# Sorting the edges of a two-layer graph network on one core: where the counts, the slot decoding, the moments and the code bits are done

## The chip, the cores and the metric

One core of a Trainium2 chip. The metric is the device time of one execution in microseconds, here the median of several. Engines are called TensorE (PE; its weight loads are PEld), VectorE (DVE), ScalarE (ACT), GpSimd (POOL) and SyncE (SP, which here only issues transfers).

## The reference

1250 nodes with 512 features, 41250 edges (sources and targets in `src` and `dst`, sorted by `dst`), one weight an edge.

```python
h = jnp.maximum(_layernorm(x, axis=-1), 0.0)
m = relu(concatenate([h[src], h[dst]], axis=1) @ W0.T + b0)     # per edge
x = x + segment_sum(m, src, num_segments=1250)
h = jnp.maximum(_layernorm(x, axis=-1), 0.0)
out = segment_sum((h @ W1.T)[src] * edge_weight[:, None], dst, num_segments=1250)
x = x + where(out >= 0, out, alpha * out)
```

## The kernel before, in words

Nodes form 10 blocks of 125, edges lie as 125 rows by 330 columns. The kernel first sorts the edges into tiles of 128 by the pair (block of the source, block of the target), 100 buckets; this is the part that the change touches. Then come the edge groups and mixed groups, which build the messages of a tile and sum them into nodes and into a 1250 x 1250 matrix M of weights, and at last the second layer's products and the output. These later stages start behind the barrier at the end of the sort and are the same in both kernels.

**The prelude of the sort.** VectorE turns node numbers into block numbers and digits (`dig_s`, `dig_d`: one-hot over blocks, L529). ScalarE regroups them, TensorE makes a histogram (L768) and totals (L773), VectorE works out the first slot of each bucket from them by a chain of some twenty short instructions (L562 to L593). The 330 columns are five chunks of 66. For each chunk `count` (L671 to L681, 66 matmuls) makes the counts of the buckets by column, ScalarE copies them to `counts_out` (`copy_counts`, L823), SyncE moves them to one row a bucket (`counts_by_bucket`, L331), VectorE runs a scan over them (`bases`, L441, with the running value of the chunk before) and splits the result in two halves, which SyncE writes as two rows into `hot`; a third row, `base_up`, comes from ScalarE. `hot_of_block` (L434) fills the other rows of `hot`. TensorE's `prefix` (L683) then gives, seven buckets at a time and 15 times a chunk, the slot of each edge in each bucket; VectorE's `pick` (L457) keeps that of the edge's own bucket, and `slots` (L473) adds the picked planes and decodes tile and lane by eleven short instructions, each of which waits for the one before. In the prelude this is done for chunk 0.

Beside it, in the prelude: VectorE makes the bits of an edge's code (L603 to L611), GpSimd the pieces of its weight (L396 to L398) and the bias rows; ScalarE the moments of x (`moments`, L874: two blocks early, eight between the first and the second half of the weights) and their square roots with one table load; TensorE turns the first layer's weights (`turn_w`, L709, eight) and takes off their rounded part (`low_w`, L718, eight), with ScalarE's two copies of each (`turned_weights`, L884). Two pairs of weights come before chunk 0's prefixes and two behind. SyncE's queue has `src`, the first two blocks of x, the weights, the rest of x, the bias, alpha, and the clearing of the table in HBM, and then the counts and rows.

**The column loop.** Of the 330 columns, 136 (`DMA_COLS`) are scattered by GpSimd into a table in HBM, one indirect transfer each (L417), chunk by chunk as soon as the slots of the chunk are ready. The other 194 (`PE_COLS`: 38 in each of the first four chunks, 42 in the last) are placed by TensorE. Column q: VectorE makes two one-hots (`column`, L495), ScalarE three scaled pieces (`pieces`, L836; in 28 columns VectorE makes these too), TensorE three matmuls (`place`, L697). A ring of six buffers lets VectorE run up to six columns ahead of `place`. All the rest is hung into this loop by hand, by column number: within a chunk, at column i, the hot blocks of the next chunk (i below 10), a clearing of the planes (i = 10), its `bases` (i = 4), `prefix` (from 9), `pick` (from 14) and all of `slots` (30), and the counts of the chunk after next in three thirds near the chunk's end (`COUNT_BACK`), with ScalarE's copy at `COPY_BACK`; and by a period of 16 columns (`STEP`), one block of the first layer: normalizing, turning, eight steps of products, two roundings.

At the end SyncE reads the table back (L351), VectorE adds it to what TensorE placed (L655) and decodes, and a barrier ends the stage.

Of the kernel before, what the change touches and what calls it, by code (L numbers as in the profile page):

```python
# [20 lines left out]
ALU = mybir.AluOpType  # L21
ACT = mybir.ActivationFunctionType
# [8 lines left out]
P = 128  # L31
N = 1250
D = 512
# [51 lines left out]
BASES_AT, PREFIX_AT, PICK_AT, SLOTS_AT = 4, 9, 14, 30  # L85

COUNT_BACK, COPY_BACK = 7, 3


STEP = 16  # L90
NORMAL_AT, TURN_AT, ROUND_AT, REST_AT, PRODUCT_AT = 2, 5, 8, 12, 13
# [14 lines left out]
def build(nc, x, src, dst, edge_weight, w0, b0, w1, alpha, out):  # L106
    rows_dram = nc.dram_tensor("edge_rows", [2, AGRP, GRP * P], BF16).ap()
    table_dram = nc.dram_tensor("edge_table", [1 + P * NT, TABLE_FIELDS], F32).ap()
    with ExitStack() as top:
# [13 lines left out]
        neg_mean = sb("neg_mean", [P, NBLK], F32)  # L123
# [19 lines left out]
        with ExitStack() as early:  # L143
# [22 lines left out]
            ones_row = early_sb("ones_row", [EROWS, NBKT], F32)  # L166
            own_base = early_sb("own_base", [NBKT, NBKT], F32)
# [9 lines left out]
        with ExitStack() as scope:  # L177
# [32 lines left out]
            ones_r = sb1("ones_r", [2, P], F32R)  # L210
            before_b = sb1("before_b", [P, P], BF16)
            keep = sb1("keep", [NBKT, CHUNK + 1], BF16)
            counts_out = sb1("counts_out", [NBLK, NBLK, CHUNK], BF16)
            counts = sb1("counts", [NBKT, CHUNK + 2], BF16)
            running = [sb1(f"running{k}", [NBKT, CHUNK + 1], F32) for k in range(2)]
            base_hi = sb1("base_hi", [NBKT, CHUNK], BF16)
            base_lo = sb1("base_lo", [NBKT, CHUNK], BF16)
            bases_at = sb1("bases_at", [NBKT, 2], F32)
# [9 lines left out]
            bias_r = sb1("bias_r", [2, D], F32R)  # L228
# [3 lines left out]
            sums = sb1("sums", [BN, 3, NBLK], F32)  # L232
# [7 lines left out]
            HALF = CHUNK // 2  # L240
            def count_ps(k):

                return [psum[0:NBLK, bank, 0:HALF * NBLK] for bank in ((0, 2) if k == 1 else (4, 5))]

# [17 lines left out]
            code_ready = sem("code_ready")  # L262
            digits_ready = sem("digits_ready")
# [14 lines left out]
            counts_in = sem("counts_in")  # L278
# [18 lines left out]
            act_own = sem("act_own")  # L297
            std_ready = sem("std_ready")
            rstd_ready = sem("rstd_ready")
# [15 lines left out]
            with nc.Block() as block:  # L315
                @block.sync
                def _(sp):
                    for rows in SPLIT:
                        sp.dma_start(src_i[rows], src.rearrange("(p c) -> p c", p=EROWS)[rows]).then_inc(src_in, 16)
                    for part, blocks in enumerate(X_PARTS):  # L320
                        for rows in SPLIT:
                            sp.dma_start(S[rows, blocks], x.rearrange("(b p) d -> p b d", p=BN)[rows, blocks]).then_inc(x_in[part], 16)
                        if part == 0:
                            sp.dma_start(w_in[:], w0.rearrange("(o p) i -> p o i", p=P)).then_inc(w_loaded, 16)
# [3 lines left out]
                    sp.wait_ge(cleared, 1)  # L328
                    sp.dma_start(table_dram[1:1 + P * NT].rearrange("(p t) f -> p (t f)", p=P),
                                 zeros.rearrange("p t f -> p (t f)")).then_inc(cleared_dram, 16)  # L330
                    def counts_by_bucket(k):  # L331
                        sp.wait_ge(count_out, k + 1)
                        if k > 0:
                            sp.wait_ge(scan_step, k)
                        sp.dma_start(counts[:, 2:CHUNK + 2], counts_out[:]).then_inc(counts_in, 16)

                    counts_by_bucket(0)
                    for k in range(NCHUNK):
                        for r, part in enumerate((base_hi, base_lo)):
                            sp.wait_ge(base_rows, 2 * k + r + 1)  # L340
                            sp.dma_start(hot[EROWS + r:EROWS + r + 1], part[:]).then_inc(rows_in, 16)
                        if k == 0:
                            sp.wait_ge(upper_row, 1)
                            sp.dma_start(hot[EROWS + 2:EROWS + 3], base_up[:]).then_inc(upper_in, 16)
# [1429 lines left out]
```

## Time and profile before

| what | us |
|---|---|
| median of 3 runs | 1008.88 (1006.73 to 1010.54) |
| the profiled execution, its own time | 1017.97 |
| its span | 1016.2 |
| mean granted TensorE clock | 0.975 |
| TensorE busy | 972.9 (96%) |
| VectorE busy | 872.2 (86%) |
| ScalarE busy | 775.0 (76%) |
| GpSimd busy | 643.0 (63%) |

The durations come from the profiled execution, which was 9.1 us longer than the median. Matmuls are pipelined and the ends of their records are modelled, so TensorE's busy share says less than the starts of its instructions. A row of a timeline gives the start, the length up to the end of the last of the merged instructions, the engine, the line, the operation, and in brackets how long the engine sat idle before it and what released it. Issuing a transfer is shown with a q behind the engine. In a row of waits stand the total, the times and the longest. The sort ends at 276.65 us of the span, the first column is placed at 52.76.

### The profile page before, as it was taken

To read this page: it belongs to the slowest core of one execution; us is meant where nothing else is said; L and a number is where in the kernel's file an instruction comes from. 1 tells how busy PE (TensorE), PEld (TensorE's weight loads), DVE (VectorE), ACT (ScalarE), POOL (GpSimd) and SP (SyncE) were. 2 spreads that over 40 slices of the span, in tenths; PEclk is the share of its full clock that TensorE was granted. 3 is DMA by queue.
4 is the path that set the end of the run, shared out by engine and by line. 5 is a ranking of instruction groups with operands and counts; after the bars stand their busy time and mean duration, and the time that the engine had idled before them with its cause. 6 is when DMAs were issued, how large, how long until landed. Compare 5 with 4: busy or idle time off the path is not lost.

```text
span 1016.2 us, 20178 instructions
## 1 busy us (share of the span) xinstructions
PE 972.9 (96%) x4719; PEld 781.0 (77%) x4720; DVE 872.2 (86%) x1747; ACT 775.0 (76%) x1650; POOL 643.0 (63%) x934
## 2 busy tenths in 40 slices
PE   5799999999799999999999999999999999999998
PEld 5477778787678887788878778878888788778776
DVE  6989988897769999999999999999999888873444
ACT  4887878778788888888888888888888776755210
POOL 2478877767477777777777777777777755530000
PEclk9689999899989999999999999999999999999999
DMA  8000000000021111111111111111111100010011
GB/s 220 4 3 4 2 4 2 4 2 3 19 62 42 44 42 41 40 42 43 41 43 42 40 40 41 43 42 41 44 41 42 31 30 30 24 42 1 21 41 40
DMA packets 35923, 35.16 MB, mean 35 GB/s; under 512 B 7778, under 2 KB 32095, under 8 KB 35876
## 3 DMA queue, kind: packets, MB, share of 16 engines
q1 hardware_dynamic: 31176, 33.95, 10.7%
q0 software_dynamic: 4416, 0.30, 1.7%
q8 instruction: 23, 0.38, 0.2%
q10 hardware_dynamic: 284, 0.33, 0.1%
q14 instruction: 24, 0.20, 0.1%
HBM read 30.92 MB, written 3.29 MB: 34 GB/s over the span
## 4 chain that ended last, share of the span: by engine, by line
PE 68%; DVE 2%; ACT 1%; issue 1%; POOL 0%; POOLq 0%
PE node_ps L1166 8%; PE edge_ps L1205 8%; PE edge_ps L1211 8%; PE edge_ps L1210 8%; PE edge_ps L1206 8%; PE node_ps L1167 8%; PE m_ps L1177 4%; PE psum L1309 3%; PE psum L1311 3%; PE psum L1310 3%; PE m_ps L1291 1%; PE edge_ps L1269 1%; PE edge_ps L1270 1%; PE edge_ps L1261 1%; PE edge_ps L1266 1%; PE edge_ps L1265 1%
## 5 line engine op out<-in xcount | busy, mean ns | idle before, releaser
L1398 ACT ACTIVATE msg_hi<-edge_ps 128x512 fp32r<-128x512 f32 x332 | 197.6, 595 | 60.8 <-PE edge_ps L1211 60.7
L1122 POOL TENSOR_TENSOR M<-M,pair_w 125x125 f32 x332 | 160.7, 484 | 126.9 <-DVE pair_w L1545 97.2
L1559 DVE SCALAR_TENSOR_TENSOR msg_lo<-edge_ps,msg_hi 128x512 fp32r<-128x512 f32 x332 | 223.6, 683 | 17.3 <-ACT msg_hi L1398 13.0
L417 POOL DMA_INDIRECT edge_table<-fields,row_no x136 | 170.4, 1253 | 58.2 <-issue 47.4
L844 ACT ACTIVATE lane_piece<-hot_lane,fields 125x128 fp32r<-125x128 bf16 x498 | 153.8, 392 | 12.1 <-DVE hot_lane L504 11.8
L705 PE MATMUL psum<-hot_tile,lane_piece 125*128 125x384 f32 x582 | 145.8, 373 | 9.2 <-ACT lane_piece L844 6.3
L1106 POOL TENSOR_TENSOR hot_w<-hot_d,weight_l 128x252 fp32r<-128x252 bf16 x166 | 140.0, 843 | 0.0
L1166 PE MATMUL node_ps<-msg_hi,hot_s 128*125 128x512 f32 x332 | 135.1, 407 | 0.0
L1205 PE MATMUL edge_ps<-b_hi,turned_d 125*128 x332 | 132.7, 400 | 0.7 <-ACT turned_d L1382 0.7
L1211 PE MATMUL edge_ps<-a_lo,turned_s 125*128 x332 | 131.9, 397 | 0.0
L1210 PE MATMUL edge_ps<-a_hi,turned_s 125*128 x332 | 131.4, 396 | 0.2 <-ACT turned_s L1382 0.2
L1206 PE MATMUL edge_ps<-b_lo,turned_d 125*128 x332 | 131.3, 395 | 0.0
L1167 PE MATMUL node_ps<-msg_lo,hot_s 128*125 128x512 f32 x332 | 130.7, 394 | 0.0
L705 PEld LDWEIGHTS psum<-hot_tile,lane_piece 125*128 125x128 f32 x582 | 106.1, 196 | 30.6 <-ACT lane_piece L844 17.1
L1373 ACT ACTIVATE square<-spread,minus_no 125x512 bf16<-125x512 bf16 x164 | 117.8, 718 | 2.7
L1540 DVE TENSOR_TENSOR S<-S,node_ps 125x512 f32 x166 | 112.7, 679 | 1.5
L502 DVE TENSOR_SCALAR hot_tile<-iota,tile_no 125x384 fp32r<-125x384 f32 x194 | 89.8, 463 | 20.6 <-PE psum L705 17.8
L1106 POOL TENSOR_TENSOR hot_w<-hot_d,weight_h 128x252 fp32r<-128x252 bf16 x166 | 101.3, 610 | 4.1 <-DVE hot_d L1550 3.1
L1390 ACT COPY pair_w<-m_ps 125x504 f32<-125x504 f32 x166 | 94.6, 570 | 0.0
L1545 DVE TENSOR_TENSOR pair_w<-pair_w 125x252 f32<-125x252 f32 x166 | 86.3, 520 | 0.0
L1166 PEld LDWEIGHTS node_ps<-msg_hi,hot_s 128*125 128x125 f32 x332 | 61.6, 185 | 25.8 <-issue 13.1
L1550 DVE TENSOR_TENSOR hot_s<-iota_h,local_s 128x504 fp32r<-128x504 f16 x96 | 75.5, 787 | 0.0
(258 smaller groups left out, 2044.8 us busy)
## 6 DMA issues: line engine op xcount, KB each, us to landing
spread<-edge_rows SPq DMA_DIRECT2D x190, 125.0 KB
out_dram<-result SPq DMA_DIRECT2D x10, 224.0 KB
edge_table<-fields,row_no POOLq DMA_INDIRECT x136
w_in<-in_L_gnn_W_dram SPq DMA_DIRECT2D x1, 2048.0 KB, 12.7
S<-in_x_dram SPq DMA_DIRECT2D x1, 1792.0 KB
w_in<-in_L_gnn_W_dram SPq DMA_DIRECT2D x1, 1024.0 KB, 5.1
S<-in_x_dram SPq DMA_DIRECT2D x1, 448.0 KB
edge_table<-zeros SPq DMA_DIRECT2D x1, 384.0 KB, 14.9
```

The costliest lines, as they stand in the source:

```text
L417: pool.indirect_dma_start(table_dram[:, :], bass.IndirectOffsetOnAxis(ap=row_no[:, c:c + 1], axis=0), fields[:, c, 0:TABLE_FIELDS], None). ...
L705: mm = pe.matmul(code_ps if f == 0 else weight_ps, lane_piece[r][:, f, :], hot_tile[r][:], start=(q == 0 and f < 2), stop=True, skip_group ...
L1106: pool.tensor_tensor(hot_w[h][:, :, f, :], hot_d[k][:, 0, h * PAIR:(h + 1) * PAIR, :], part[:, bass.ds(g * GRP + (MIXC + h * PAIR), PAIR)] ...
L1122: pool.tensor_tensor(part, part, pair_w[h][:, j, 0, 0:BN], ALU.add).then_inc(m_added, 1)
L1166: pe.matmul(sums[:], hot_s[k][:, j, 0:BN], msg_hi[j][:], start=(j % PAIR == 0), stop=False)
L1167: pe.matmul(sums[:], hot_s[k][:, j, 0:BN], msg_lo[j][:], start=False, stop=(j % PAIR == PAIR - 1)).then_inc(tile_summed, 1)
L1205: pe.matmul(edge_ps[j][:], td, b_hi[:, b_rows], start=True, stop=False)
L1206: pe.matmul(edge_ps[j][:], td, b_lo[:, b_rows], start=False, stop=False)
L1210: pe.matmul(edge_ps[j][:], ts, a_hi[:, a_rows], start=False, stop=False)
L1211: pe.matmul(edge_ps[j][:], ts, a_lo[:, a_rows], start=False, stop=True).then_inc(edge_ready, 1)
L1398: act.activation(msg_hi[j][:], edge_ps[j][:], ACT.Relu).then_inc(hi_ready, 1)
L1559: dve.scalar_tensor_tensor(out=msg_lo[j][:], in0=edge_ps[j][:], scalar=0.0, in1=msg_hi[j][:].bitcast(F32), op0=ALU.max, op1=ALU.subtract). ...
```

## The change

Counts and bases. All counts get room of their own (`counts_out`, `counts`, `running` over all 330 columns). The counts of chunks 2, 3 and 4 are made behind columns 0, 1 and 2 of chunk 0 (`COUNTS_AT`), copied by ScalarE two columns later, always as two halves; the bases of chunk 1 are scanned at column 1, those of chunks 2 to 4 in one scan of 198 columns at column 12 (`BASES_AT`). SyncE writes the rows of a chunk when the picks of the chunk before are done. Prefixes start at column 8 and wait only for the hot blocks that they read.

Slots. `slots` is cut into ten steps, two a column, from column 30 to 34; the wait for the last is at the chunk's last column. The first pick of a later chunk is a product of prefix and one-hot, so that the planes aren't cleared.

Moments. VectorE makes them with two statistics instructions a block, and the reciprocal and shift block by block; block 0 in the prelude, block b at stages 2, 3, 11 and 12 of the 16 columns before its own; ScalarE takes one root a block, and its table for roots is loaded at the start.

Code bits. GpSimd makes them in nine instructions instead of VectorE's five, from the moment the pairs are known, and then the weight pieces as before.

Order. The weights are loaded on ScalarE's queue, the table is cleared from GpSimd's, the rest of x is loaded behind chunk 0's rows of bases. After the first pair of weights, TensorE does one of the twelve other parts of weights behind each of prefixes 1 to 12. The bias is multiplied with 128 rows instead of 2, of which all but two are zero.

```diff
-BASES_AT, PREFIX_AT, PICK_AT, SLOTS_AT = 4, 9, 14, 30
-COUNT_BACK, COPY_BACK = 7, 3
+WEIGHTS_FROM, COUNTS_AT, COPIES_BEHIND = 1, (0, 1, 2), 2
+BASES_AT, PREFIX_AT, PICK_AT, SLOTS_AT = (1, 12), 8, 14, 30
+SLOT_STEPS, STEPS_A_COLUMN = 10, 2
+MOMENTS_AT, STD_AT = (2, 3, 11, 12), 4
...
                     counts_by_bucket(0)
-                    for k in range(NCHUNK):
...
+                    counts_by_bucket(1)
+                    rows_of_bases(0)
+                    sp.wait_ge(upper_row, 1)
+                    sp.dma_start(hot[EROWS + 2:EROWS + 3], base_up[:]).then_inc(upper_in, 16)
+                    load_x(1)
+                    rows_of_bases(1)
+                    for k in range(2, NCHUNK):
+                        counts_by_bucket(k)
+                    for k in range(2, NCHUNK):
+                        rows_of_bases(k)
...
+                    pool.wait_ge(pairs_ready, 1)
+                    pair_of, part, upper_bits = blk_a[:, 1, :], local[:, 1, :], local[:, 0, :]
+                    own(pool.tensor_scalar(part, node_f[:, 0, :], float(TILE), None, ALU.mult))
+                    own(pool.tensor_tensor(upper_bits, part, node_f[:, 1, :], ALU.add))
...
+                        if k > 0 and g == 0:
+                            dve.tensor_tensor(planes[:, 0:nb, :].rearrange("p b c -> p (b c)"), psum[0:EROWS, 3 + n % 3, 0:nb * CHUNK],
+                                              hot[0:EROWS, 0:nb, :].rearrange("p b c -> p (b c)"), ALU.mult).then_inc(picked, 1)
...
+                    def moment(b, stage):
+                        if stage == 0:
+                            dve.wait_ge(x_in[0 if b < X_PARTS[0].stop else 1], 32)
+                            dve.bn_stats(stats[:, b, :], S[0:BN, b, :]).then_inc(moments, 1)
+                            return
+                        dve.wait_ge(moments, 4 * b + stage)
+                        if stage == 1:
+                            dve.bn_aggr(mv[:, b, :], stats[:, b, :]).then_inc(moments, 1)
...
-                    weights(1)
                     for g in range(NPICK):
                         prefix(0, g)
-                    weights(2)
-                    weights(3)
+                        if WEIGHTS_FROM <= g < WEIGHTS_FROM + 12:
+                            weights_part(4 + g - WEIGHTS_FROM)
...
-                            part = i - last + COUNT_BACK
-                            if k + 2 < NCHUNK and 0 <= part < 3:
-                                count(k + 2, range(CHUNK // 3 * part, CHUNK // 3 * (part + 1)))
+                            if k == 0 and i in COUNTS_AT:
+                                count(COUNTS_AT.index(i) + 2)
```

## Rows read from the trace of the kernel before

**Rows 1.** The page, part 4: the chain that ended last, shares by engine.

```profile
PE 68%; DVE 2%; ACT 1%; issue 1%; POOL 0%; POOLq 0%
```

**Rows 2.** Busy time by stretch of the column loop; PE, PEld, DVE, ACT, POOL, PEclk.

```profile
86.64:132.31 45.67, 43.60 (x268) 36.10 (x268) 41.67 (x119) 38.46 (x117) 34.89 (x28) 1.00 0.09 3
132.31:179.12 46.81, 44.34 (x268) 36.70 (x267) 40.12 (x119) 38.52 (x117) 35.26 (x28) 0.96 0.08 3
179.12:227.68 48.56, 47.28 (x272) 38.95 (x271) 41.90 (x120) 38.70 (x118) 35.79 (x28) 0.93 0.08 3
227.68:271.94 44.26, 42.35 (x204) 33.83 (x202) 34.87 (x101) 37.98 (x122) 29.81 (x24) 1.00 0.10 11
```

**Rows 3.** Timeline of TensorE before the first column: start us, us, instruction.

```profile
29.70 0.85 PE L693 MATMUL psum<-hot,before_b 128*125 128x462 bf16 x3 [1.44 <-DMA hot<-base_up]
...
46.05 3.79 PE L714 MATMUL psum<-ident,w_in 128*128 128x128 f32 x16 [0.19 <-ACT w0T_lo L890]
...
49.49 0.77 PE L721 MATMUL psum<-w0T_hi,minus_ident 128*128 128x512 f32 x1
...
52.76 2.99 PE L705 MATMUL psum<-hot_tile,lane_piece 125*128 125x384 f32 x9 [1.65 <-issue]
```

**Rows 4.** Timeline of ScalarE, the same stretch.

```profile
42.46 1.28 ACT L906 ACT_TABLE_LOAD   x1
...
51.63 2.74 ACT L844 ACTIVATE lane_piece<-hot_lane,fields 125x128 fp32r<-125x128 bf16 x9
```

**Rows 5.** Timeline of VectorE, the same stretch.

```profile
24.78 0.36 DVE L447 TENSOR_TENSOR_SCAN running<-keep,bases_at,counts 100x67 f32<-100x67 bf16 x1 [4.24 <-DMA counts<-counts_out]
...
30.12 8.10 DVE L469 COPY_PREDICATED planes<-hot,psum 125x462 f32<-125x462 uint16 x15 [0.32 <-PE psum L693]
...
38.25 1.90 DVE L480 TENSOR_REDUCE slot<-planes 125x66 f32<-125x924 f32 x1
...
42.41 0.23 DVE L492 SCALAR_TENSOR_TENSOR row_no<-lane,tile_no 125x66 int32<-125x66 f32 x1
```

**Rows 6.** Timeline of SyncE's DMA issues, the same stretch.

```profile
16.18 0.94 SPq L335 DMA_DIRECT2D counts<-counts_out  x1
...
26.99 0.74 SPq L344 DMA_DIRECT2D hot<-base_up  x1
```

**Rows 7.** GpSimd's weight pieces and first scatter; all scatters of the loop grouped.

```profile
31.59 1.05 POOL L398 TENSOR_TENSOR fields<-weight,fields 125x330 f32<-125x330 f32 x1
...
43.66 1.29 POOL L417 DMA_INDIRECT edge_table<-fields,row_no  x1 [7.47 <-issue]
...
L417 POOL DMA_INDIRECT edge_table<-fields,row_no x131 | 164.0, 1252 | 49.6 <-issue 38.7 <-DVE row_no L492 10.9
```

**Rows 8.** End of the loop: SyncE's read of the table, its wait, VectorE's first use.

```profile
266.19 0.34 SPq L351 DMA_DIRECT2D raw<-edge_table  x1
...
SPq L315 <- DMA raw<-edge_table: 2.5, 1, 2.5
...
271.94 0.56 DVE L655 TENSOR_TENSOR raw<-raw,psum 128x384 f32<-128x384 f32 x1 [2.78 <-PE psum L705]
```

**Rows 9.** GpSimd beside a two-input VectorE instruction, and after it.

```profile
277.41 0.97 POOL L1106 TENSOR_TENSOR hot_w<-hot_d,weight_h 128x252 fp32r<-128x252 bf16 x1 [3.09 <-DVE hot_d L1550]
...
278.91 0.60 POOL L1106 TENSOR_TENSOR hot_w<-hot_d,weight_h 128x252 fp32r<-128x252 bf16 x1
```

**Rows 10.** Counts in chunks one and two: ScalarE's wait, TensorE's wait, one third of counts.

```profile
140.11 0.70 ACT L833 CAST counts_out<-psum 10x660 bf16<-10x660 f32 x1 [3.04 <-remote]
...
142.21 0.79 PE L705 MATMUL psum<-hot_tile,lane_piece 125*128 125x384 f32 x3 [2.06 <-ACT lane_piece L844]
...
180.38 0.75 PE L678 MATMUL psum<-dig_d,dig_s 125*10 125x10 bf16 x22
```

**Rows 11.** Two microseconds behind the counts of chunk two, columns as in rows 2.

```profile
184.00:186.00 2.00, 2.00 (x5) 1.12 (x6) 1.68 (x7) 2.00 (x7) 1.39 (x3) 0.50 0.06 1
```

**Rows 12.** Statistics by VectorE in the last stage, grouped.

```profile
L1625 DVE BATCH_NORM_STATS2 stats<-S 125x6 f32<-125x512 f32 x10 | 6.8, 682 | 0.0
```

More of the change, by code:

```diff
@@ new lines, in slots @@
+                        dve.wait_ge(vstep, steps[0])
+                        if step == 1:
+                            mark(dve.tensor_scalar(quotient, slot[:], -MID_SLOT, 1.0 / UPPER, ALU.add, ALU.mult))
+                        if step == 2:
+                            mark(dve.tensor_scalar(upper, quotient, MAGIC, -MAGIC, ALU.add, ALU.add))
+                        if step == 3:
+                            mark(dve.scalar_tensor_tensor(out=slot[:], in0=upper, scalar=-UPPER, in1=slot[:], op0=ALU.mult, op1=ALU.add))
@@ new lines, in slots @@
+                        if step == 4:
+                            mark(dve.tensor_scalar(quotient, slot[:], -(TILE - 1) / 2, 1.0 / TILE, ALU.add, ALU.mult))
+                        if step == 5:
+                            mark(dve.tensor_scalar(whole, quotient, MAGIC, -MAGIC, ALU.add, ALU.add))
+                        if step == 6:
+                            mark(dve.tensor_tensor(after, whole, upper, ALU.subtract))
+                            mark(dve.scalar_tensor_tensor(out=at, in0=whole, scalar=-float(TILE), in1=slot[:], op0=ALU.mult, op1=ALU.add))
@@ new lines, in slots @@
+                        if step == 7:
+                            mark(dve.tensor_scalar(in_mix[:], after, float(MID_TILE), None, ALU.is_equal))
+                            mark(dve.scalar_tensor_tensor(out=tile, in0=after, scalar=float(MID_TILE), in1=whole, op0=ALU.is_le, op1=ALU.add))
+                        if step == 8:
+                            mark(dve.copy_predicated(tile, in_mix[:].bitcast(U16), mix_no[:, cols]))
+                        if step == 9:
+                            dve.scalar_tensor_tensor(out=row_no[:, cols], in0=at, scalar=float(NT), in1=tile, op0=ALU.mult,
+                                                     op1=ALU.add).then_inc(slots_ready, 1)
@@ L645, in _ @@
                                         pick(k + 1, g)
-                                if i == SLOTS_AT:
-                                    slots(k + 1)
+                                for step in range(SLOT_STEPS):
+                                    if i == SLOTS_AT + step // STEPS_A_COLUMN:
+                                        slots(k + 1, step)
+                                if i == FIRST[k + 1] - FIRST[k] - 1:
                                     dve.wait_ge(slots_ready, k + 2)
@@ L770, in _ @@
                     mm.then_inc(hist_done, 1)
[L771 removed]
+                    count(0)
                     pe.wait_ge(spread_done, 1)
```

267 lines of the change are left out of this document (122 added, 145 removed).

## The prediction

> **What bounds the kernel now.** I read the chain that ended last first [rows 1]: 68% of the span is TensorE's. The edge and mixed groups and the output blocks behind 276.65 us are not touched by the change, and I carry their time over unchanged. What can move is the sort: a prelude until the first column is placed, and 194 columns after it.
>
> In the column loop the table of busy time by stretch shows that no engine is far ahead [rows 2]. The four stretches go from one decoding of slots to the next, the last one to the end of the loop. TensorE is busy 42 to 47 us of each, but VectorE 40 to 42 and ScalarE 38 to 39 of the first three: whoever is late by more than the ring of six columns stops the others.
>
> The prelude is a relay. TensorE's first prefix starts at 29.70 [rows 3], with a wait for the row that SyncE loads last; the second half of the turned weights runs up to the first column at 52.76. ScalarE does the moments and a table load of 1.28 us at 42.46 before it copies these weights out, and only at 51.63 makes the first pieces of a column [rows 4]. VectorE waits 4.24 us for the first counts, picks from 30.12, reduces from 38.25 and issues the last step of the first decoding at 42.41, so ends it at 42.64 [rows 5]. On SyncE the counts are issued at 16.18, behind all of x, the weights and the clearing of the table; the last row of bases is issued at 26.99 [rows 6].
>
> One more engine must be read, though it never stops the others: GpSimd. It does the weight pieces from 30 us on, issues its first scatter at 43.66 and then 136 in all; those of the loop take (164.0 + 38.7) / 131 = 1.547 us each with the gap of issue, and only 10.9 us are waits for slots [rows 7]. The table is read back at 266.19 and has landed after 2.5 us of waiting, at about 269.0; VectorE needs it at 271.94, where TensorE's last column releases it [rows 8]. So GpSimd's chain has 2.9 us of slack at the end of the loop, and no more.
>
> **The change part by part.**
>
> *Transfers.* x's second part moves behind the first rows of bases on SyncE, the weights go to ScalarE's queue (one issue more, while ScalarE would wait for digits), the clearing of the table to GpSimd's (about 1 us of issue, in time that GpSimd has idle). The counts' transfer then has little ahead of it. I give it the 2.7 us that the last row took from its issue to the prefix it released (26.99 to 29.70) [rows 3, 6]: landed at 18.9. VectorE's wait of 4.24 [rows 5] goes to zero, and everything behind it in this relay moves by 4.2: first prefix at 25.5. The bound for this part is 0 (another load ahead still holds it) to -4.2.
>
> *Code bits by GpSimd.* Nine instructions of 125x330 at most 1.05 us each [rows 7], so 8 to 10 us from 13 us on; with the weight pieces done by 25, where nothing waits for them before the first column. VectorE loses five, 2.6 us, in a stretch where it waits for the prefix anyway: 0. What it may cost is the neighbour. An operation of GpSimd takes 0.97 us beside a VectorE instruction that reads two operands from SBUF, and 0.60 us alone [rows 9]; the loser here is GpSimd. The other direction isn't isolated by a row. VectorE has some 12 such short dependent instructions from 14 to 20.5 us. I take +1.0 us for all of them (a tenth of an operation each), with ends 0 and 12 x 0.5 = +6, half an operation each. First prefix: 26.5.
>
> The Trainium skill ("SBUF — State Buffer", Who interferes with whom) speaks against this placing: a VectorE instruction with two SBUF inputs and a GpSimd one that reads SBUF exclude each other for the whole instruction, and whoever issues first blocks the other. By that rule the upper end holds, and it is a rival below.
>
> *Weights between the prefixes.* This is the step that costs. Before, 15 prefixes were bound by the picks, 8.10 / 15 = 0.54 us each [rows 5], and twelve parts of weights came partly behind. Now all twelve parts lie between prefixes 1 and 13. Two turns take 49.49 - 46.05 = 3.44 us, six take 10.3; six roundings are shown at 0.77 alone, I take 0.5 each in a row, 3.0; a prefix takes 0.85 / 3 = 0.28, I take 0.33 with handovers, 5.0 [rows 3]. Sum 18.3 us (ends 16.0 and 10.3 + 4.6 + 8.1 = 23.0). The last prefix ends at 44.8, its pick at 45.3, and the decoding takes 42.64 - 38.25 = 4.4 [rows 5], nothing being there to lie between: 49.7, which is 7.1 us later than before. ScalarE's moments, table load and late weight copies [rows 4] fall away, so the first pieces no longer wait for them: decoding 49.7, about 0.8 for the first two one-hots (an estimate; GpSimd's first scatter, which the same decoding releases, came 1.0 behind it) [rows 7], pieces 1.1 (51.63 to 52.76) [rows 3, 4], first column placed at 51.6 against 52.76. The gain of the prelude is 1.2 us for TensorE, and a loss of 7.1 us for GpSimd.
>
> *Counts.* Three sets (198 matmuls) leave the ends of chunks 0 to 2 and go behind columns 0 to 2. A third of a set is 0.75 us [rows 10], a set 2.1. At the loop's start ScalarE gives a column each 2.74 / 3 = 0.91 us [rows 4], and TensorE waits for it; my estimate is that 2 or 3 of the 6.4 us fill this idle time, and that ScalarE's three copies, queued ahead of its next pieces, add a little. I take +3.0 for the first stretch (ends +1, +5). In chunk one ScalarE waited 3.04 us for its copy of the counts and TensorE 2.06 for the pieces then missing [rows 10]; behind the counts of chunk two the clock fell to the lower level, 0.50 granted (1.2 of 2.4 GHz) [rows 11]; three windows of 2 us in a row look like this one, so some 3 us were lost. Taken from the first three stretches of [rows 2]: counts 2.1 + 2.1 + 2.1, TensorE's stall 2.1, the clock 1.1 (half may come back elsewhere). That is 9.5, and the ends are 6 and 12.
>
> *Slots in ten steps, picks.* The eleven instructions behind the reduction take 42.64 - 40.15 = 2.5 us, each waiting for the one before [rows 5]; spread, I take half, -1.2. The first pick of a chunk multiplies and so needs no clearing, and two of three scans are merged away with their roundings: about -1.2 (an estimate, at 0.36 for a scan [rows 5]). *Moments:* statistics take 0.68 us a block [rows 12], with three small ones about 1.1, and a chunk has 38 / 16 blocks: +2.6. VectorE comes out even; I take 0 (ends -3, +3). The bias product with 128 rows instead of 2 streams as many columns: 0.
>
> *Sum.* TensorE: 51.6 + (271.9 - 52.8) + 3.0 - 9.5 = 264.2. GpSimd: first scatter 1.0 behind the decoding, at 50.7; 136 x 1.547 = 210.4, no wait for slots since a chunk of 28 takes it 43.3 us; end 261.1, read 1.2 later, landed 2.8 after: 265.1. **The two ends are within 1 us of each other**, GpSimd's is the floor, and any slip of either counts, so I take 266.5, against 271.94: -5.4 us. The profiled execution took 1017.97 (span 1016.2 and 1.8 around it), 9.1 above the median 1008.88; its changed twin would take 1012.6. The same difference on the median gives **1003.5 us**. About 0.5%, 5 us, is what a measurement of this kernel can tell from no change, so this forecast lies at the edge.
>
> **The rivals.**
> *A shorter prelude.* If prefixes and roundings take their lower ends (16.0) and the neighbour costs nothing, decoding ends at 46.4, GpSimd at 261.8 and TensorE with 12 us saved at 260: about -9.5, 999.4. For it: TensorE is then never idle; against it: the clock stood at the lower level there before.
>
> *The port.* VectorE's chain is held by 6 instead of 1 us: decoding ends at 54.7, GpSimd's chain at 270.1: -1.8 and 1007.1. For it is the rule above, against it that the rows show GpSimd as the one delayed.
>
> *VectorE or ScalarE bounds the loop.* The counts' time is not given back, as VectorE's 40 us a chunk, its wait at column 12 for the transfers of three counts and the ring of six columns set the pace: 4 of the 9.5 us are saved, the loop ends at 269.7: -2.2, 1006.7. For it: VectorE's busy time is within 2 to 5 us of TensorE's [rows 2].
>
> *Slower: the scatters.* GpSimd starts 7 us later and now has no slack. If VectorE's denser stream stretches its cycle, every 0.1 us costs 13.6. From 1.60 us on the gain is gone; at 1.65 the chain ends at 50.7 + 224.4 + 4.0 = 279.1, +7.2 and 1016.1. For it: GpSimd's busy time of 28 scatters rose from 34.89 to 35.79 over three chunks; against it: that is 0.03 us each [rows 2].
>
> **How the numbers follow.** Forecast 0.50 (1001 to 1005.5; 0.36 beyond 0.5%, 0.14 within), shorter prelude 0.10, port 0.15, VectorE's bound 0.13, scatters 0.12. Faster 0.36 + 0.10 = 0.46; same 0.14 + 0.15 + 0.13 = 0.42; slower 0.12. The range takes in the forecast, port, VectorE's bound and most of the shorter prelude, with 1 to 2 us of scatter between runs: 998 to 1011. It leaves out the slower scatters and the far end of the short prelude.
>
> **What would show it.** The first scan of bases near 20.6 without a wait; first prefix at 25 to 27; turned weights between prefixes and the last prefix near 45; first scatter near 50.7, scatters without waits for slots, and the table's arrival, not TensorE's last column, as what releases VectorE near 266; no stall at the counts in chunk one. The forecast is wrong if the first scatter comes later than 55, if the mean cycle of the scatters is above 1.6, or if TensorE's last column ends behind 268.

## The result, and the profile after

| | median, us | lowest to highest | runs |
|---|---|---|---|
| kernel before | 1009.47 | 1005.21 to 1012.43 | 20 |
| changed kernel | 1012.60 | 1010.07 to 1014.19 | 20 |

Ratio 1.003, 95% interval 1.002 to 1.0041: slower by 3.1 us, or 0.3%. The forecast of 1003.5 had the wrong sign, and the result lies outside its range. The profiled execution of the changed kernel took 1012.84 us (span 1011.1, mean clock 0.981) and is typical of its runs. That of the kernel before took 1017.97, 5.5 above the longest of these 20 runs. So a second and a third profile of the kernel before were taken (`before_again`, 1008.76 us, and `before_third`, 1011.44). The rows below are set against `before_again`, in places against `before_third` too.

Busy time by stretch of the changed kernel, columns as in [rows 2]: from one decoding of slots to the next, the end of the loop, the stage behind the barrier.

```profile
49.23:93.20 43.97, 42.43 (x364) 36.93 (x365) 40.52 (x120) 35.14 (x110) 34.43 (x28) 0.83 0.10 5
93.20:134.76 41.56, 39.59 (x196) 33.21 (x195) 41.39 (x126) 37.67 (x118) 33.33 (x27) 1.00 0.08 3
134.76:177.06 42.30, 40.28 (x204) 33.77 (x202) 41.89 (x127) 38.76 (x120) 34.07 (x28) 1.00 0.09 3
177.06:218.18 41.12, 40.74 (x206) 35.42 (x207) 40.66 (x124) 38.03 (x118) 33.19 (x27) 1.00 0.08 3
218.18:266.88 48.70, 39.19 (x192) 31.98 (x190) 32.76 (x93) 34.78 (x113) 35.72 (x29) 0.95 0.10 10
...
271.88:1011.10 739.22, 727.41 (x3310) 581.30 (x3310) 638.25 (x1069) 558.61 (x1007) 459.24 (x765) 0.99 0.12 38
```

The same table of `before_again`:

```profile
81.36:126.41 45.05, 43.31 (x268) 36.09 (x268) 40.93 (x119) 38.58 (x117) 36.21 (x29) 1.00 0.09 3
126.41:172.06 45.65, 44.21 (x272) 36.27 (x272) 41.33 (x119) 38.71 (x117) 36.81 (x29) 1.00 0.09 3
172.06:219.24 47.18, 45.44 (x271) 37.60 (x270) 41.90 (x121) 38.46 (x117) 38.03 (x30) 0.96 0.09 3
219.24:263.52 44.28, 42.05 (x202) 33.47 (x200) 34.83 (x101) 38.01 (x122) 29.80 (x24) 1.00 0.10 11
...
268.20:1007.10 738.90, 727.44 (x3310) 582.61 (x3310) 638.59 (x1069) 558.84 (x1007) 461.90 (x765) 0.99 0.12 38
```

The stage behind the barrier takes 739 us in both, so the difference is made in the sort. The three middle stretches did get shorter, by 3.5, 3.4 and 6.1 us (4.1, 3.3 and 4.4 against `before_third`). The first stretch, taken up below, is 10.8 us longer, and the last one 4.4: 48.7 us with 39.2 of TensorE's work in it. The end of the sort shows what holds the last one. Changed kernel: VectorE's first use of the table, TensorE's last columns, GpSimd's last scatter, SyncE's read of the table, and all scatters grouped as in [rows 7].

```profile
266.88 0.55 DVE L707 TENSOR_TENSOR raw<-raw,psum 128x384 f32<-128x384 f32 x1 [10.63 <-DMA raw<-edge_table]
...
245.89 12.72 PE L754 MATMUL psum<-hot_tile,lane_piece 125*128 125x384 f32 x60 [0.56 <-ACT lane_piece L885]
...
261.25 1.17 POOL L444 DMA_INDIRECT edge_table<-fields,row_no  x1 [0.30 <-issue]
...
263.83 0.36 SPq L360 DMA_DIRECT2D raw<-edge_table  x1
...
L444 POOL DMA_INDIRECT edge_table<-fields,row_no x136 | 171.7, 1262 | 61.0 <-issue 59.4 <-DVE row_no L535 1.6
```

And in `before_again`, with TensorE's first column ahead:

```profile
48.18 5.79 PE L705 MATMUL psum<-hot_tile,lane_piece 125*128 125x384 f32 x18 [1.65 <-ACT lane_piece L844]
...
263.52 0.56 DVE L655 TENSOR_TENSOR raw<-raw,psum 128x384 f32<-128x384 f32 x1 [2.81 <-PE psum L705]
...
250.74 12.74 PE L705 MATMUL psum<-hot_tile,lane_piece 125*128 125x384 f32 x60 [0.56 <-ACT lane_piece L844]
...
255.12 1.23 POOL L417 DMA_INDIRECT edge_table<-fields,row_no  x1 [0.31 <-issue]
...
257.76 0.34 SPq L351 DMA_DIRECT2D raw<-edge_table  x1
...
POOL edge_table L417 <- DVE row_no L492: 0.4, 1, 0.4
```

Before, TensorE's last column releases VectorE, at 263.5, and the table had landed 2.8 us earlier, at 260.7 (read issued from 257.76 to 258.10, then 2.6 of waiting). After, TensorE is done at 245.89 + 12.72 = 258.6, 4.9 earlier than in `before_again` and 7.1 earlier than in `before_third`, and VectorE then sits idle for 10.63 us, until the table is there. **The sort now ends at GpSimd's chain of 136 scatters**, whose end, the issue of the read behind the last scatter, moved from 257.8 to 263.8: 3.9 us by its later start (first scatter at 48.30, in `before_again` at 44.41), 1.2 by waits for slots (1.6 against 0.4) and 1.0 by the scatters themselves (from the first one's start to the last one's end, less these waits, 212.5 against 211.5). From there to the landing it is as long as before.

VectorE's first use of the table is thus the mark of every run below: 271.94 in the profile shown before [rows 8], 263.52 and 265.76 in the other two of the same kernel, 266.88 after. From the mark to the end of the span it was 740.9 to 744.3 us in the fourteen profiles of this document, so a difference between two marks gives that between two whole times only to within some 3 us.

The prelude of the changed kernel, where TensorE's rows answer to [rows 3]:

```profile
29.29 1.00 PE L742 MATMUL psum<-hot,before_b 128*125 128x462 bf16 x2 [3.08 <-DVE hot L464]
...
35.01 1.11 PE L763 MATMUL psum<-ident,w_in 128*128 128x128 f32 x8
35.95 0.36 PE L742 MATMUL psum<-hot,before_b 128*125 128x462 bf16 x1
...
41.63 0.42 PE L742 MATMUL psum<-hot,before_b 128*125 128x462 bf16 x2
49.23 1.30 PE L754 MATMUL psum<-hot_tile,lane_piece 125*128 125x384 f32 x3 [7.17 <-ACT lane_piece L885]
```

VectorE's scan, reduction and last decoding step, as in [rows 5], and GpSimd's first scatter, as in [rows 7]:

```profile
23.61 0.75 DVE L473 TENSOR_TENSOR_SCAN running<-keep,running,counts 100x66 f32<-100x66 bf16 x1
...
42.91 1.89 DVE L513 TENSOR_REDUCE slot<-planes 125x66 f32<-125x924 f32 x1
...
47.05 0.23 DVE L535 SCALAR_TENSOR_TENSOR row_no<-lane,tile_no 125x66 int32<-125x66 f32 x1
...
48.30 1.30 POOL L444 DMA_INDIRECT edge_table<-fields,row_no  x1 [18.59 <-issue]
```

The scan no longer waits for the counts but comes only 1.2 earlier than in [rows 5]; the prefixes end at 42.05, the slots are decoded at 47.28. TensorE has its first column at 49.23 (48.18 in `before_again`).

### The profile page after: what moved, and what is told of

Its sections match the earlier page's. It is cut to its first block, busy times and chain, and to the rows that moved or that the text cites. A ratio compares the mean times of both kernels' runs of the same rounds, so it can differ in the third digit from the quotient of the medians.

```text
span 1011.1 us, 20245 instructions
## 1 busy us (share of the span) xinstructions
PE 955.0 (94%) x4719; PEld 774.3 (77%) x4720; DVE 877.9 (87%) x1770; ACT 760.9 (75%) x1621; POOL 655.2 (65%) x946
## 4 chain that ended last, share of the span: by engine, by line
PE 69%; DVE 2%; ACT 1%; issue 0%; POOL 0%; POOLq 0%
PE node_ps L1190 8%; PE edge_ps L1234 8%; PE edge_ps L1229 8%; PE edge_ps L1235 8%; PE edge_ps L1230 8%; PE node_ps L1191 8%; PE m_ps L1201 4%; PE psum L1333 3%; PE psum L1335 3%; PE psum L1334 3%; PE m_ps L1315 1%; PE edge_ps L1293 1%; PE edge_ps L1294 1%; PE edge_ps L1289 1%; PE edge_ps L1285 1%; PE edge_ps L1290 1%
## 5 line engine op out<-in xcount | busy, mean ns | idle before, releaser
L545 DVE TENSOR_SCALAR hot_tile<-iota,tile_no 125x384 fp32r<-125x384 f32 x194 | 93.8, 483 | 8.5 <-PE psum L754 8.4
L1569 DVE TENSOR_TENSOR pair_w<-pair_w 125x252 f32<-125x252 f32 x166 | 84.0, 506 | 0.0
L1190 PEld LDWEIGHTS node_ps<-msg_hi,hot_s 128*125 128x125 f32 x332 | 61.5, 185 | 27.0 <-issue 13.6
## 6 DMA issues: line engine op xcount, KB each, us to landing
w_in<-in_L_gnn_W_dram ACTq DMA_DIRECT2D x1, 2048.0 KB, 11.9
```

Of the source, the lines that this page charges most:

```text
L1190: pe.matmul(sums[:], hot_s[k][:, j, 0:BN], msg_hi[j][:], start=(j % PAIR == 0), stop=False)
```

## The experiments

Ratios are to the kernel before on the same chip in the same session. Its medians were 1010.18 (beside `before_again`, `prefix_first`, `bits_vector`, `scatter_132`), 1008.50 (`slots_whole`, `before_132`, `counts_prelude`, `three`) and 1010.52 us (`bits_132`, `three_132`, `scatter_128`, `before_third`). Each variant was profiled once, so a mark is that of one execution.

### Is the first profile typical?

No edit: the kernel before again.

> The kernel before, unchanged, profiled once more. My theory: the profiled execution on which the prediction rests was an unlucky one (1017.97 us against 1005 to 1012 in 20 others), and the time lost lay in the column loop (TensorE's stall and two stretches at the lower clock). Expected: an execution of 1007 to 1011 us, VectorE's first use of the table (line 655) at 262 to 266 us instead of 271.9, little or none of the lower clock between 140 and 192 us, and behind the barrier 739 to 740 us again. Rival: the sort takes as long as in the first profile and the difference lies behind the barrier or around the span; then line 655 stands near 271 us again.

> The kernel before, unchanged, profiled a third time. Theory: the column loop of the kernel before ends where TensorE's columns end, and this varies from execution to execution by some us with stalls and with the stretches at the lower clock; VectorE's first use of the table at 261 to 267, execution 1006 to 1012 us, the stage behind the barrier 739 to 740 us. Rival (the first profile was typical of profiled executions): 270 us or more, and 1015 us or more.

Measured 1008.76 and 1011.44 us; the first use of the table came at 263.52 and 265.76, both times released by TensorE, with waits for slots of 0.4 and 4.1 us in place of 10.9. So 8.4 of the 9.1 us between the first profile's span and that of `before_again` lie ahead of that use: 4.6 ahead of TensorE's first column (52.76 in [rows 3], 48.18), the rest in the loop. Three stretches show the loss, columns as in [rows 2]. First the profile shown before, then `before_again`:

```profile
46.05:49.49 3.44, 3.44 (x17) 3.44 (x17) 3.30 (x12) 1.02 (x2) 2.83 (x3) 0.50 0.07 1
...
132.00:148.00 16.00, 13.91 (x116) 10.96 (x115) 11.98 (x38) 12.00 (x38) 12.65 (x10) 0.89 0.08 4
180.00:192.00 12.00, 12.00 (x98) 9.48 (x97) 8.02 (x25) 9.15 (x28) 9.87 (x8) 0.72 0.09 4
```

```profile
40.00:48.20 8.20, 5.44 (x29) 3.95 (x28) 7.79 (x29) 6.92 (x14) 3.18 (x3) 0.91 0.03 1
...
132.00:148.00 16.00, 15.23 (x84) 12.41 (x81) 14.02 (x45) 14.85 (x45) 12.95 (x11) 1.00 0.09 4
180.00:192.00 12.00, 12.00 (x60) 10.50 (x58) 10.68 (x31) 9.02 (x27) 9.56 (x9) 0.94 0.09 4
```

The turns of the weights ran at a granted clock of 0.50, where `before_again` had 0.91 on the way to its first column. The slow turns alone don't make a long execution: in `before_third` the same sixteen matmuls took 3.78 us, as long as in [rows 3], and its first column came at 51.00. The stall of 3.04 us at ScalarE's copy of the counts, and TensorE's of 2.06 [rows 10], were seen in that execution only. In `before_again` the same copy waits 1.26, in `before_third` 1.21:

```profile
132.42 0.70 ACT L833 CAST counts_out<-psum 10x660 bf16<-10x660 f32 x1 [1.26 <-PE psum L678]
```

What follows: what made that profile long lay ahead of the mark, on TensorE's path through the sort, which is the path that the change shortens. Part of the expectation was wrong, as it put all of the loss in the column loop.

### Do the scatters set the end?

Four columns of the last chunk are placed by TensorE instead of scattered: 132 scatters, 198 columns.

```diff
-... + ["DAADVADADAV" * 6]
+... + ["DAADVADAAAVDAADVADADAVDAAVVADADAVDAADVADAAAVDAADVADADAVDAAVVADADAV"]
```

In the changed kernel:

> The changed kernel with 132 scattered columns instead of 136; four columns of the last chunk are placed by TensorE instead, pieces by ScalarE for two of them and by VectorE for two. Theory (GpSimd's chain is the end): it gets 4 x 1.55 = 6.2 us shorter, TensorE's last column moves from 258.6 to about 262, which then is the end: VectorE's wait for the table falls from 10.6 us to 0 to 1, the time is 4 to 5 us shorter, near 1008 us. Rival (TensorE's and ScalarE's columns are the end, and the 10.6 us are a slip of that execution): 3 us longer, near 1015 us.

In the kernel before:

> The kernel before with the same 132 scattered columns that made the changed kernel 7 us faster. Theory (in the kernel before TensorE's columns set the end, with GpSimd's table arrived about 2.5 us ahead of it): four more columns are four times 0.6 to 1.1 us more on the path, 2.5 to 4 us longer, 1012 to 1014 us. Rival (both kernels are held by the scatters): 4 to 6 us shorter, 1004 to 1006 us.

Measured: 1005.48 (ratio to before 0.9961, interval 0.9944 to 0.9979), 7.1 below the changed kernel and more than the 4 to 5 expected; and 1010.20 in the kernel before (1.0016, 0.9996 to 1.0035), no gain. Of the 7.1 us the mark shows 4.9; the profiled executions are 6.4 apart, and the rest of that lies behind the mark. The first use of the table in `scatter_132`:

```profile
261.95 0.56 DVE L707 TENSOR_TENSOR raw<-raw,psum 128x384 f32<-128x384 f32 x1 [2.35 <-PE psum L754]
```

In `before_132`:

```profile
265.15 0.56 DVE L655 TENSOR_TENSOR raw<-raw,psum 128x384 f32<-128x384 f32 x1 [2.31 <-PE psum L705]
```

The same edit pays only where GpSimd's chain is last. `before_132` is inconclusive as to the price of four columns more (+1.7 us in the median, less than its interval is wide), but excludes the 4 to 6 us that fewer scatters alone would have gained had the scatters set its end. Eight fewer in the changed kernel:

> The changed kernel with 128 scattered columns. Theory: the crossing of the two ends lies near 132; from there on TensorE's columns are the end, which move by 0.85 us each: VectorE's first use of the table at 265 to 266 after a wait for TensorE, with GpSimd's table there at 255, and the time 1008 to 1009.5 us, 3 to 4 longer than with 132. Rival (scatters are the end throughout): 6 us shorter than with 132, 999 us.

Measured 1006.40 (0.9969, 0.9953 to 0.9985), below the 1008 to 1009.5 expected. It is 0.9 above `scatter_132` in another session, which the two intervals don't tell apart, but VectorE is released by TensorE at 263.84, 1.9 later. With 132 the bound has already passed back to TensorE; taking eight columns from the scatters brings nothing more than taking four.

### What makes GpSimd start late?

`prefix_first`: all 15 prefixes in a row, the twelve parts of weights behind them.

```diff
                         prefix(0, g)
-                        if WEIGHTS_FROM <= g < WEIGHTS_FROM + 12:
-                            weights_part(4 + g - WEIGHTS_FROM)
+                    for n in range(4, 16):
+                        weights_part(n)
```

> The changed kernel with its fifteen prefixes of chunk 0 in a row and the twelve parts of weights behind them. Theory (GpSimd's chain of 136 scatters sets the end of the sort, so what counts is when the first slots are decoded): picks again at 0.54 us each, decoding done near 42.5 instead of 47.3, first scatter near 43.5, VectorE's first use of the table near 262, and the time 4 to 5 us shorter than the changed kernel's, near 1008 us. Rival (TensorE's columns set the end): the first column is placed no earlier than 49.2 as the weights now lie ahead of it, and the time stays at 1012 to 1013 us.

Measured 1010.82 (1.0009, 0.9998 to 1.002), 1.8 below the changed kernel where 4 to 5 were expected. The first scatter came at 43.9, 4.4 earlier, but the table was used at 266.02, only 0.9 earlier, because the slots of chunk 1, ready at 92.4, were now what GpSimd waited for:

```profile
POOL edge_table L444 <- DVE row_no L535: 5.2, 1, 5.2
```

`bits_vector`: the code bits back on VectorE, behind the hot blocks of the prelude.

```diff
-                    pool.wait_ge(pairs_ready, 1)
-                    own(pool.tensor_scalar(part, node_f[:, 0, :], float(TILE), None, ALU.mult))
...
+                    own(dve.scalar_tensor_tensor(out=upper_bits, in0=node_f[:, 0, :], scalar=float(TILE), in1=node_f[:, 1, :],
+                                                 op0=ALU.mult, op1=ALU.add))
...
```

> The changed kernel with the code bits made by VectorE again, in the place where the kernel before has them. Theory (the code bits on GpSimd hold up VectorE's chain from 16 to 23.6 us, 3.1 us): the first scan of bases at 20.6 instead of 23.6, first prefix near 26.5, first scatter near 46, the time 2 to 3 us shorter, 1010 us. Rival (the chain is late for another reason, or VectorE's five instructions, 2.6 us, come in the way of the picks): first scatter within 0.7 us of 48.3 and the time 1012 to 1013 us.

Measured 1008.19 (0.9986, 0.9973 to 1.0), 4.4 below the changed kernel where 2 to 3 were expected. The scan came at 20.54 instead of 23.61, the first prefix at 25.46 instead of 29.29, the first scatter at 43.9, and the table was used 3.6 earlier:

```profile
263.26 0.55 DVE L707 TENSOR_TENSOR raw<-raw,psum 128x384 f32<-128x384 f32 x1 [10.59 <-DMA raw<-edge_table]
```

Here both what opens the chain and what feeds it came earlier, as TensorE had its first column at 44.9; the wait for slots stayed at 1.6. The chain of scatters still ends last, by 8 us.

### Is TensorE's gain in the loop hidden?

`slots_whole`: all ten steps of the decoding at one column, as before.

```diff
-SLOT_STEPS, STEPS_A_COLUMN = 10, 2
+SLOT_STEPS, STEPS_A_COLUMN = 10, 10
```

> The changed kernel with all ten steps of a decoding at column 30 again (one number changed). Theory (GpSimd's chain is the end and now waits once, 1.6 us, for the slots of chunk 1): these slots come a little earlier, the wait falls to 0 to 1, TensorE's last column comes 2 to 5 us later than 258.6 and is still covered by the scatters; the time stays within 1.5 us of the changed kernel's 1012.6. Rival (the decoding in one piece costs what TensorE loses): 1015 us or more.

Measured 1011.46 (1.002, 1.0005 to 1.0035), 1.1 below the changed kernel, a difference that the intervals don't show to be one. TensorE's last column ends 7.1 us later than with the steps spread, where 2 to 5 were expected, and the sort ends no later:

```profile
265.76 0.56 DVE L707 TENSOR_TENSOR raw<-raw,psum 128x384 f32<-128x384 f32 x1 [2.54 <-PE psum L754]
...
253.01 12.72 PE L754 MATMUL psum<-hot_tile,lane_piece 125*128 125x384 f32 x60 [0.56 <-ACT lane_piece L885]
```

The column loop of TensorE, from its first to its last column, takes 215.9 us here and 209.4 in the changed kernel. GpSimd had its slots without any wait (chunk 1's at 89.6 instead of 93.2), its read of the table was issued at 261.58 instead of 263.83, and TensorE's columns were the last to end (265.7, with the table there at 264.4). Spreading the decoding is worth 6.5 us of TensorE's time in these two profiles, more than the 1.2 a chunk that the prediction gave it in VectorE's, and delays what GpSimd needs by 3.6.

`counts_prelude`: the counts of chunks 2 to 4 in TensorE's idle time ahead of the first column, and ScalarE's copies of them ahead of column 0 and at columns 0 and 1 (not in the cut shown).

```diff
+                    pe.wait_ge(picked, NPICK)
                     pe.wait_ge(count_out, 2)
+                    pe.wait_ge(w_lo, 2 * KC)
+                    for k in range(2, NCHUNK):
+                        count(k)
...
-                            if k == 0 and i in COUNTS_AT:
-                                count(COUNTS_AT.index(i) + 2)
...
```

> The changed kernel with the counts of chunks 2 to 4 in the stretch where TensorE idles while VectorE decodes the first slots, instead of behind columns 0 to 2. Theory (the scatters are the end; the first starts at 48.3 whatever the counts do, and only the 1.6 us waited for the slots of chunk 1 can be had): slots of chunk 1 at 88 to 91 instead of 93.2, TensorE's last column near 254, the time 1 to 2 us shorter, 1011 us. Rival (TensorE's work decides): 4 to 6 us shorter, 1007 us.

Measured 1011.90 (1.0025, 1.0011 to 1.0039), 0.7 below the changed kernel and not clear of noise; TensorE's last column ended at 257.2, where 254 was expected. Chunk 1's slots came at 91.2, 2.0 earlier, and GpSimd's wait for them went away, but its first scatter came at 49.1 and the table was used at 266.81, as before the edit. The place of the counts makes chunk 1's slots 2 us late, and alone does not set the end.

### A version that beats both

`three` joins `bits_vector`, `prefix_first` and `counts_prelude`; `bits_132` is `bits_vector` with 132 scatters, `three_132` is `three` with 132.

> The changed kernel with three parts moved together: code bits by VectorE, the prefixes in a row ahead of the weights, the counts of chunks 2 to 4 ahead of the first column. Theory (what counts are the first slots, and then the slots of chunk 1, as GpSimd waits for nothing else): first slots decoded near 38.5, first scatter near 39.5, a wait for the slots of chunk 1 of 2 to 6 us remains, VectorE's first use of the table at 258 to 261, and the time 1003 to 1006 us. If the parts only took each other's place (prefixes first alone gave 1.8 us of the 4.4 by which its first scatter was earlier), it would be 1008 as with the code bits alone.

> The changed kernel with two things altered that each shortened GpSimd's chain: code bits by VectorE, and 132 scattered columns instead of 136. Theory (two ends, GpSimd's scatters and TensorE's columns, the later one counts): from the profiles of each alone the table is there at 263.3 - 6.2 = 257.1, TensorE's last column is done at 255.1 + 3.4 = 258.5; the time is 1003 to 1004.5 us, 4 to 5 below the code bits alone and 1 to 2.5 below the 132 columns alone. Rival (the gains don't add up as one chain was meant): 1005.5 us, as with 132 columns alone.

> The kernel with three parts moved together (code bits by VectorE, prefixes in a row, counts ahead of the first column) and 132 scattered columns. Theory: table there at 261.7 - 6.2 = 255.5, TensorE's last column at 253.5 + 3.4 = 257, so VectorE's first use of the table near 257 and the time 1001 to 1003 us. Rival: as GpSimd waits 4 us for the slots of chunk 1 there, the scatters saved in the last chunk still count in full, but TensorE, which placed its first column only at 51.1, slips to 260: 1005 us.

| kernel | first scatter | table used | TensorE's last column | median (runs) | ratio to before, interval |
|---|---|---|---|---|---|
| changed | 48.3 | 266.88 | 258.6 | 1012.60 (20) | 1.003, 1.002 to 1.0041 |
| three | 40.1 | 261.71 | 253.5 | 1006.14 (12) | 0.997, 0.9954 to 0.9986 |
| bits_132 | 44.2 | 257.62 | 257.5 | 1001.98 (6) | 0.9923, 0.9898 to 0.9949 |
| three_132 | 39.9 | 254.98 | 254.9 | 998.86 (6) | 0.9893, 0.9869 to 0.9916 |

`three` came out at the slow end of what was expected (1003 to 1006), the two others 1 and 2 us below theirs (1003 to 1004.5, 1001 to 1003). `three_132` is 1.1% faster than the kernel before:

```profile
254.98 0.56 DVE L707 TENSOR_TENSOR raw<-raw,psum 128x384 f32<-128x384 f32 x1 [2.35 <-PE psum L754]
...
236.92 18.03 PE L754 MATMUL psum<-hot_tile,lane_piece 125*128 125x384 f32 x81
```

Joined, the scatters start 8.4 us earlier than in the changed kernel, of which a wait of 4.0 for slots takes a part, and the four columns moved to TensorE bring the two ends within 1 us of each other. In `bits_132` they are balanced as well: the last scatter starts at 251.7, and the table lands as TensorE ends.

## Why the prediction was wrong

**Where it failed.** In the last step of its sum: "The same difference on the median gives 1003.5 us". Read as a forecast of the changed kernel's own profile it was close: the table used at 266.5 (measured 266.88), the changed twin at 1012.6 us (the profiled execution took 1012.84, the median is 1012.60). Part of this is luck. Against the sum's 265.1 for GpSimd, the start came 2.4 us earlier, while waits for slots (1.6), longer scatters (2.1) and the landing (0.5) added 4.2; the forecast's 266.5 holds 1.4 us on top, for slips. But the 9.1 us by which the profile of before exceeded the median were subtracted from the twin too. They were not a constant that both kernels carry. They were made on TensorE's path through the sort, and the change takes that path's end out of what ends last and puts a chain of scatters there, which varies less: less its waits it took 210.2 to 211.5 us in the three profiles of the kernel before, and 211.2 to 213.4 in the six of the changed kernel and its variants with 136 scatters. The prediction had the floor of that chain and wrote that GpSimd's is the floor; a floor is an absolute time in the span, to be compared with where the sort usually ends. That was to be had from the numbers at hand: if all of the 9.1 lay ahead of the mark (8.4 did), the usual end was 271.94 less 9.1, 262.8, and a floor of 266.5 is 3.7 above it (2.3 by the 265.1 without the slips). Measured: 3.1 slower. The spread of the runs fits: 7.2 us before, 4.1 after. None of the prediction's three signs of being wrong came up (first scatter at 48.3, not behind 55; 1.562 us a scatter, not 1.6; TensorE's last column at 258.6, not behind 268), since none of them looked at where the sort of the kernel before usually ends.

**The counts.** Right: no wait, and the transfer isn't late. Without the code bits on GpSimd (`bits_vector`) the first scan came at 20.54, the 4.2 us earlier that were forecast, and the first prefix at 25.46, where 25.5 was.

**The code bits, mis-sized.** Taken at +1.0 with an end at +6; measured +3.1 at the first scan (23.61, 20.54 with the bits on VectorE) and +3.8 at the first prefix (29.29 and 25.46). The rival of the port was right about the mechanism and gave it 6 us; the next part but one shows the rows.

**Weights between the prefixes, mis-sized.** Taken at 18.3 us (ends 16.0 and 23.0), measured 42.05 - 29.29 = 12.8. The price of the turns was taken from a stretch at the lower clock level. A turn of eight matmuls starts at 35.01 and the next prefix at 35.95, so 0.94 us, and four of the six are like it; the other two, the first ones, took 1.71 and 1.46, which no row explains, as the clock was granted in full from 29.29 to 42.05. The forecast used 1.72, half of the 3.44 in [rows 3], where it stood at 0.50. With 0.94 its own sum gives 13.6 (an estimate). The same sixteen matmuls in `before_again`, to set beside the 3.79 in [rows 3]:

```profile
43.30 2.05 PE L714 MATMUL psum<-ident,w_in 128*128 128x128 f32 x16 [0.19 <-ACT w0T_lo L890]
```

The errors of code bits and weights nearly cancel in the decoding (49.7 forecast, 47.28 measured; it took 4.37 from its reduction on, 4.4 forecast), and GpSimd's first scatter came at 48.3 instead of 50.7.

**The loop.** The three middle stretches gained 12.9 us against `before_again` (11.9 against `before_third`, 16.1 against [rows 2]), where 9.5 with ends 6 and 12 were forecast; the undersized term is the spread decoding, for which the prediction gave VectorE 0 in all. With the decoding in one piece (`slots_whole`) the same three stretches are 7.3 us longer. VectorE is busy for 41.39 of 41.56 us there, so it seems to bound the loop now, though no run takes work off it: the rival that named it gave 4 us where 12.9 were saved. The first stretch was forecast at +3.0. It is 43.97 us long against 33.2 in `before_again` (48.2 to 81.4), +10.8: 3.6 because the last step of the decoding lies four columns later (the last stretch gets these back), the rest the counts (2 us by `counts_prelude`) and, as far as can be read, the clock. TensorE was idle for 7.17 us ahead of the first column. The clock fell to 0.50, the lower level, at 47, while it was idle, and rose again at 64. Columns as in [rows 2], changed kernel, then `before_again`, then `prefix_first`:

```profile
42.05:49.23 7.18, 0.01 (x2) 0.04 (x1) 6.77 (x22) 1.50 (x5) 0.93 (x1) 0.84 0.00 0
49.23:62.00 12.77, 12.77 (x218) 11.06 (x219) 10.39 (x33) 9.11 (x29) 10.34 (x9) 0.50 0.13 10
```

```profile
48.20:62.00 13.80, 13.30 (x56) 9.91 (x57) 13.62 (x42) 13.29 (x44) 11.19 (x9) 0.88 0.09 4
```

```profile
52.00:64.00 12.00, 12.00 (x195) 10.72 (x192) 5.71 (x17) 8.27 (x26) 9.69 (x8) 0.50 0.11 7
```

With twelve parts of weights gone from behind the prefixes nothing was left for TensorE to do while VectorE decodes. But the idle time is not shown to be what the clock cost: in `prefix_first` TensorE had the weights to do there and was granted 1.00, and the clock fell all the same once the counts and first columns ran, to 0.50 from 52 to 64; with the counts ahead of the first column (`counts_prelude`) it stood at 0.50 from 49.2 to 58. What made chunk 1's slots late for GpSimd is shown better: its wait of 1.6 us goes away with the decoding in one piece (slots 3.6 earlier) or with the counts in the prelude (2.0 earlier), and it grows to 5.2 where the first scatter comes 4.4 earlier and these slots only 0.8.

From its first to its last column TensorE took 209.4 us, 5.9 less than in `before_again` (5.3 less than in `before_third`), where the sum had +3.0 - 9.5 = -6.5. That it fits is luck too: a first stretch 7.8 worse than forecast, 3.6 of that given back in the last, against middle stretches 3.4 better. Its end at 258.6, 5.6 earlier than forecast, was worth nothing.

**The scatters.** 136 at 1.562 us, 1.547 forecast: +2.1 us. The rival in which denser work of VectorE slows them by 0.1 us each did not come about; they were 0.015 slower. The slower kernel that it forecast came about by another cause. Its first sentence, "GpSimd starts 7 us later and now has no slack", was right in kind (3.9 us later than in `before_again`), but set against the long execution it seemed to need slower scatters as well to end on the wrong side.

**Not tried.** The moments back on ScalarE alone, the order of the transfers alone, and the new place of the counts in the kernel before. How the rest of the loop's gain splits among them stays open.

## What to carry to other kernels

Before a difference of rows is carried onto a median, compare the profiled execution with the spread of the runs; if it lies outside, profile again, and find out which stretch holds the excess. Where a change replaces what ends last by something else, don't subtract: set the new chain's absolute end against where the stage ends in a typical execution. And where two engines share a job (here columns and scatters), moving one engine's start calls for a new split: the same four columns were worth 7.1 us in the median with the change and nothing that shows without it.

## What the runs showed of the hardware that wasn't expected

In three places a short VectorE instruction with two inputs lasted until GpSimd's long one beside it ended. VectorE in the changed kernel, then GpSimd at the same time:

```profile
17.27 0.66 DVE L626 TENSOR_TENSOR zt<-tiles_of 125x50 f32<-125x50 f32 x1
...
20.69 0.72 DVE L636 TENSOR_TENSOR zt<-tiles_to,tiles_of 125x100 f32<-125x100 f32 x1
...
24.63 1.10 DVE L478 TENSOR_TENSOR base_lo<-running,base_hi 100x66 bf16<-100x66 f32 x1
```

```profile
17.03 0.84 POOL L414 TENSOR_TENSOR local<-local 125x330 f32<-125x330 f32 x1
...
20.52 0.77 POOL L418 TENSOR_TENSOR local<-local 125x330 f32<-125x330 f32 x1
...
24.48 1.18 POOL L425 TENSOR_TENSOR fields<-weight,fields 125x330 f32<-125x330 f32 x1
```

Each of VectorE's ends within 0.12 us of GpSimd's (17.93 and 17.87, 21.41 and 21.29, 25.73 and 25.66). The same three in `bits_vector`, where GpSimd is idle:

```profile
17.03 0.21 DVE L614 TENSOR_TENSOR zt<-tiles_of 125x50 f32<-125x50 f32 x1
...
19.02 0.26 DVE L624 TENSOR_TENSOR zt<-tiles_to,tiles_of 125x100 f32<-125x100 f32 x1
...
21.15 0.23 DVE L466 TENSOR_TENSOR base_lo<-running,base_hi 100x66 bf16<-100x66 f32 x1
```

The Trainium skill ("SBUF — State Buffer", Who interferes with whom) says that the two exclude each other for the whole instruction and that issue order decides who waits; the trace agrees, with 0.21 to 0.66, 0.26 to 0.72 and 0.23 to 1.10 us. What such an instruction pays is what is left of the long one, so a chain of short, dependent ones pays again and again. Ones with one input paid as well in places: that at 16.50 took 0.49 instead of 0.19 us, and the one at 17.97 the same, though it ended half a microsecond before GpSimd's did. In all it is 3.1 us over the some twenty of this chain, which the forecast had at a tenth of an instruction each.
